# Causal attention with its units in another order: query chunks 1 and 2 in turn, then 3 and 0

## What is computed

```python
qkv = x @ w_qkv.T
q, k, v = jnp.split(qkv, 3, axis=-1)
q, k, v = (reshape(q), reshape(k), reshape(v))      # (1, 16, 2048, 8)
q, k = _apply_rope(q, cos, sin), _apply_rope(k, cos, sin)
scores = jnp.einsum('bhsd,bhtd->bhst', q, k) / scale
scores = jnp.where(causal[None, None], scores, -jnp.inf)
attn = jax.nn.softmax(scores, axis=-1)
out = jnp.einsum('bhst,bhtd->bhsd', attn, v)
return out.transpose(0, 2, 1, 3).reshape(B, S, D) @ w_out.T
```

## Time and profile before

| | |
|---|---|
| time, median of 3 runs | 1884.07 us (1877.11 to 1885.36) |
| the profiled execution's own time | 1888.39 us |
| its span | 1886.5 us |
| granted TensorE clock, mean over the span | 0.894 |
| busy: PE, weight loads, DVE, ACT, POOL | 92%, 42%, 61%, 61%, 4% |
| causal attention, first reduction to last accumulator copy | 55.81 to 582.77 us |
| attention of layer 1, last accumulator copy | 1590 us |

### The profile page before, as it was taken

The page is one execution under the profiler, slowest core; times in us unless marked ns, Lnnn a source line. Parts: engine busy times, 40 slices in busy tenths (PEclk is TensorE's granted clock), DMA queues, the critical chain, the costliest instruction groups (busy, mean ns, idle before and its releaser), DMA issues. The chain is left out here.

```text
span 1886.5 us, 31101 instructions
## 1 busy us (share of the span) xinstructions
PE 1735.7 (92%) x12744; PEld 799.2 (42%) x12744; DVE 1159.0 (61%) x1566; ACT 1157.5 (61%) x2092; POOL 81.4 (4%) x158
## 2 busy tenths in 40 slices
PE   6889999999998999676999999999999999599999
PEld 3444433433335444332333333333333334467776
DVE  7566677788614110359898899999999852411111
ACT  3446667668784222240788888888888887133433
POOL 3110101000000000020000000000000000000000
PEclk9567788889898999775899999999999999689999
DMA  3100000000000000100000000000000000010000
GB/s 100 62 1 1 1 1 1 1 1 1 1 1 1 1 0 0 53 1 0 1 1 2 1 1 1 2 1 1 2 1 1 2 1 1 1 35 19 14 22 22
DMA packets 16763, 17.07 MB, mean 9 GB/s; under 512 B 2994, under 2 KB 13695, under 8 KB 16127
## 3 DMA queue, kind: packets, MB, share of 16 engines
q1 hardware_dynamic: 16639, 15.32, 2.6%
HBM read 14.26 MB, written 1.05 MB: 8 GB/s over the span
## 5 line engine op out<-in xcount | busy, mean ns | idle before, releaser
L559 DVE TENSOR_REDUCE maxp<-banks 128x2 f32<-128x1024 f32 (+3 forms) x800 | 943.5, 1200 | 214.1 <-PE banks L430 107.9
L539 ACT ACTIVATE probs<-banks 128x512 f32<-128x512 f32 (+3 forms) x1664 | 855.6, 571 | 242.7 <-PE banks L442 220.9
L455 PE MATMUL banks<-probs,V 128*9 128x256 f32 (+3 forms) x6272 | 508.9, 398 | 7.0 <-POOL probs L508 6.1
L442 PE MATMUL banks<-Q,K 64*128 64x512 f32 (+3 forms) x1664 | 466.3, 507 | 27.8 <-ACT Q L524 20.6
L423 PE MATMUL banks<-K,Q 64*128 64x512 f32 (+3 forms) x1664 | 394.3, 453 | 28.8 <-DVE maxp L559 27.9
L442 PEld LDWEIGHTS banks<-Q,K 64*128 64x128 f32 x1664 | 191.5, 194 | 411.1 <-ACT probs L539 305.4
L423 PEld LDWEIGHTS banks<-K,Q 64*128 64x128 f32 x1664 | 188.1, 210 | 81.8 <-DVE maxp L559 64.8
L455 PEld LDWEIGHTS banks<-probs,V 128*9 128x9 f32 x6272 | 93.6, 89 | 257.9 <-ACT probs L539 188.7
L951 DVE SCALAR_TENSOR_TENSOR x<-banks,wts,x 128x128 f32<-128x128 f32 x128 | 36.0, 344 | 198.1 <-PE banks L914 198.1
L939 ACT ACTIVATE work<-banks,eb 128x512 f32<-128x512 f32 x128 | 86.3, 687 | 105.2 <-PE banks L905 102.8
L914 PEld LDWEIGHTS banks<-work 128*128 128x128 f32 x1024 | 118.1, 192 | 11.5 <-issue 11.5
(11 more groups left out here) (126 smaller groups left out, 861.3 us busy)
## 6 DMA issues: line engine op xcount, KB each, us to landing
tables<-in_tables SPq DMA_DIRECT2D x2, 2048.0 KB, 9.7
work<-in_ew SPq DMA_DIRECT2D x16, 256.0 KB, 3.0
flex<-in_h SPq DMA_DIRECT2D x2, 1024.0 KB, 8.1
x<-in_x SPq DMA_DIRECT2D x4, 256.0 KB, 4.3
out<-x SPq DMA_DIRECT2D x4, 256.0 KB, 2.3
cst<-in_consts SPq DMA_DIRECT2D x1, 865.0 KB, 6.1
flex<-in_w SPq DMA_DIRECT2D x3, 256.0 KB, 3.0
flex<-in_w_qk SPq DMA_DIRECT2D x1, 256.0 KB, 5.9
```

Source lines behind the costliest of these rows:

```text
L442: mm = pe.matmul(ebank(e)[:, first:CW], k.K[rows, 2 * g + b, kt * P:(kt + 1) * P], k.Q[rows, n % 3, b, first:CW], start=True, stop=True)
L455: mm = pe.matmul(acc[32 * j:32 * j + HD + 1, low:high], k.V9[:, kt, g * HG + j, :], k.probs[:, slot + j, low:high], start=(kt == 0), stop= ...
L539: act.activation(k.probs[:, HG * (s % 2) + j, first:CW], ebank(e)[:, first:CW], ACT.Exp, scale=scale).then_inc(e_done, 1)
L559: dve.tensor_reduce(dst, src, AX.X, ALU.max).then_inc(m_done, 1)
```

## The change

The list of units of the causal layer is built from pairs of chunks: for each group of heads chunk 1 and then chunk 2, eight units in all; then for each group chunk 3 and then chunk 0. As `take_acc` used the position in the list as its slot in `k.outT`, it now computes the slot from chunk and group. The list for layer 1 is the old one. Everything else follows from the list.

```diff
--- before.py
+++ after.py
@@ -307,7 +307,8 @@
 
     causal = layer == 0
     scale = SCALE0 if causal else SCALE1
-    units = [(c, g) for c in range(C) for g in range(G)]
+    orders = ((1, 2), (3, 0)) if causal else ((c,) for c in range(C))
+    units = [(c, g) for order in orders for g in range(G) for c in order]
     NU = len(units)
     steps = [TC * (c + 1) if causal else T for c, g in units]
 
@@ -587,7 +588,7 @@
 
             def take_acc(n):
                 dve.wait_ge(pv_done, s_base[n + 1])
-                dve.tensor_copy(k.outT(n), acc).then_inc(acc_free, 1)
+                dve.tensor_copy(k.outT(units[n][0] * G + units[n][1]), acc).then_inc(acc_free, 1)
 
             def segment(n):
                 acc_after = sum(len(slot) for slot in plan(n + 1)[:2]) if 0 <= n < NU - 1 else 0
```

## The result

The changed kernel takes 1893.86 us (median of 7 runs, 1887.74 to 1898.33), the kernel before 1877.74 (7 runs, 1862.79 to 1886.09, the three of the prediction among them). The ratio is 1.0131, with a 95% interval of 1.0087 to 1.0176: slower, by 16 to 33 us. The two medians alone give 1.0086, at the interval's lower end, and timed again later, beside other kernels, the ratio was 1.0085 (1.0050 to 1.0121). The forecast was slower by 20.9 us, a ratio of 1.0111, and 1905 us with a range of 1884 to 1924.

What follows compares the result with a forecast made beforehand. Early units were taken as bound by PE at its lower clock, late ones by ACT and DVE in turn. Start +23.1 and units -2.2 gave +20.9 on 1888.39, 1909.3; 4.3 lower for a median: 1905 us, range 1884 to 1924.

Steps and rivals of the forecast that it cites:

- The start, +23.1: Ahead of the first exponential: 24 full and 6 edge reductions instead of 10 edge, 33.9 us instead of 10.8.
- Nothing hides it: At the start: ACT's shift copy and first exponential wait for the PE transposition behind all these reductions.
- The units, -2.2: The 16 causal attention units, priced per reduction by chunk: 508.7 us against 510.9.
- Chunk 0: Three chunk-0 units with 2 full and 10 edge reductions: 22 us each; the last, without reductions, 12.
- lower bound of 9.40: Last chunk-0 unit, without reductions: at least ACT's 9.40 us, at most 15.0, forecast 12.
- The end: Last units: filling two nearly reduction-free chunk-3 units gives little, at 0.16 us a full reduction; the one left takes 38.7.
- inherit the clock: Chunk-0 units keep the dense chunk-3 unit's clock, taking 16 us instead of 22: -18, 1887 us; chance 0.17.
- The second rival: Alternation raises PE's clock in chunk-1 and chunk-2 units to 0.92: -34, 1871 us; chance 0.08.
- a sign against itself: Forecast falls if chunk-1 and chunk-2 units come several us under 29.7 and 34.6 at a clock above 0.85.
- the third rival: Low clock spreads: unit 0 costs about 5 more, three chunk-3 units 4 more each: +17, 1922 us; chance 0.18.
- The sum: Whole kernel: +23.1 at the start and -2.2 in the units make +20.9 us, median 1905.

Runs made afterwards that it cites:

- the three profiles with that start: Profiles of the changed kernel, its repeat, and the kernel before with one unit each of chunks 1 and 2 moved first; ratios 1.0131, 1.0085, 1.0073.
- the second profile: The changed kernel timed and profiled again, nothing altered; 1.0085 of the kernel before, units 489.2 us.
- the order 1, 2, 0, 0, 0, 0: Kernel before with one chunk-1 and one chunk-2 unit moved first, the rest in old order, no alternation; ratio 1.0073.
- the filled starts: Extra 512-column matmul pairs behind each reduction ahead of the first exponential: in the changed kernel 1.0054, in the kernel before 0.9966, both against the kernel before.
- The first alternation alone: Kernel before with only chunks 1 and 2 in turn, between four chunk-0 units first and four chunk-3 units last; ratio 0.9979.
- the four profiles with 23 us more: Changed kernel twice (1.0131, 1.0085), kernel before with a chunk-1 and a chunk-2 unit moved first (1.0073), kernel before with 20 extra start reductions (1.0071).
- the three profiles with a filled start: Extra matmul pairs among start reductions of the changed kernel (1.0054), the kernel before (0.9966), and it with only chunks 1 and 2 alternating (0.9978).

## Why the prediction was right

- *The start, +23.1.* Right in size and in mechanism: +23.1, +23.1, +23.1 in the three profiles with that start, 24 full reductions at 1.14. That the first exponential came at 95.7 and not 93 is the later first reduction.
- *Nothing hides it.* Right: ACT idled 34.22 us.
- *The units, -2.2.* The sign was right and the size was off: -10.5 in the first profile, -22 in the second. The step that failed is the pricing of a reduction by differences between units at unlike clocks. Chunk 1: 26.5, 28.3 and 26.9, a mean of 27.2, for a predicted 29.7; the 1.5 us for a diagonal reduction was read from units at 0.79 and 0.75 and at 0.60 and 0.50, and two more of them cost 0.5 together, at 0.76 to 0.81. Chunk 2: 34.6 predicted, 35.6, 31.5, 34.2, and 31.5 to 31.6 in the second profile. Chunk 3: 42.2 predicted, 45.8, 41.1, 45.0. The two values belong to two clocks, not to two loads. The unit with 28 reductions took 37.84 (37.5 predicted), that with 2 full and 10 diagonal 36.07 (35.0).
- *Chunk 0.* Right: 21.0, 22.7 and 21.1 for 22, at 0.52 to 0.67. The last one took 9.60 and not 12. Its lower bound of 9.40 was misread: ACT was busy 6.02 us in it, for the 9.40 of the other chunk-0 units hold work for the units that follow.
- *The end.* Two chunk-3 units without reductions were no treasure; the one left took 37.28 at a clock of 1.00, for 38.7.
- *The rivals.* Chunk-0 units behind chunk-3 ones ran at 0.52 to 0.67 and did not inherit the clock; in the order 1, 2, 0, 0, 0, 0 one ran at 1.00 (11.11 us), so such a unit can. The Trainium skill (TensorE: Matmul & The Clock Gate, Part 1) has activity release the throttle: the filled starts at 0.83 and 0.74 agree, the unit of 16.05 us at 0.50 with PE busy 15.98 does not. The second rival came in part: the chunk-2 units went from 0.825 to 0.85, 1.00 and 0.90, and to 0.99 or 1.00 in the second profile, 3 us under their forecast, which the prediction had named as a sign against itself; the chunk-1 units only from 0.755 to 0.76, 0.80 and 0.81. Beyond the forecast the units gave 8 us in the first profile and 20 in the second, of the rival's 34, not enough to pay for the start. The first alternation alone gave 0.9979 with 1 inside the interval, so what the Trainium skill (Perfetto Trace Analysis, Optimization Strategy) says of interleaved regimes was not to be seen here in the time. Of the third rival, chunk-3 units behind sparse ones were at 0.86 and 0.88 in two of three cases; they took 6.4 us more than forecast, and the one at 1.00 gave 1.1 back (131.9 together, 126.6 predicted). Unit 0 did not come out longer.
- *The sum.* +20.9 against 16.1 between the medians and 24.6 by the ratio. It was right partly by balance: the profile's start and units give +12.6 and the two profiled executions differ by 9.6. The profile of before, from which the sum was made, lay near the top of that kernel's range, so its units had a lower clock than most runs. The median of 1893.86 lies 11 under the forecast of 1905, just below the forecast's own 1895 to 1915; the range of 1884 to 1924 holds it because it takes in two rivals as well.

## What to carry to other kernels

Count first what a reordering leaves uncovered ahead of the first consumer; this term could be read from two rows, held to 0.1 us in the four profiles with 23 us more, and it decided the sign. A gain that is priced by comparing stages of one profile must be compared at the same granted clock, or the clock's price is taken for the work's. And moving work from the open into a unit is only a gain where that unit has room at the clock it gets: here DVE's busy time alone looked like the limit, and the unit took 45.06 us where it said 37 to 40, with PE at 0.63.

## What was not expected of the hardware

- The length of a unit of given content goes with its clock: 31.5 us at 1.00, 34.2 at 0.90 and 35.6 at 0.85 for chunk 2 with 20 reductions, 41.1 at 1.00 and 44.9 to 45.0 at 0.88 for chunk 3 with 24. The first two came back in different kernels to 0.1 us; others lie between (32.19 at 0.97).
- The same program's mean clock ran from 0.893 to 0.918 over its runs, and its time over 35 us, 1.9%: more than the change under study.
- A PE that was busy 21.72 of 23.91 us stayed at 0.50. The start of the changed kernel, busy 25.6 of 37.4, was at 0.50 too, and with pairs of 512-column matmuls in its gaps it was at 0.83 with 27.85 busy. Busy time in the records does not tell which level is granted.
- In the three profiles with a filled start the level fell from 1.00 to 0.50 within the 2.2 us in which PE had no matmul, just before unit 0.
